# Latent attention with a pair's keys in one tile and each head's score products in half of TensorE's rows

## What is computed

```python
k_eff = (Wdq.T @ Wuq.T @ Wuk).reshape(nh, hs, Lkv)          # nh = 16, hs = 16, Lkv = 64
v_eff = (Wuv.T @ Wo.T).reshape(Lkv, nh, hs).transpose(1, 0, 2)
c_kv = x @ Wdkv.T
q = (x @ Wdq.T @ Wuq.T).reshape(B, T, nh, hs).transpose(0, 2, 1, 3)
q_lat = jnp.einsum('bhtd,hdl->bhtl', q, k_eff)
scores = jnp.einsum('bhtl,bsl->bhts', q_lat, c_kv) / jnp.sqrt(jnp.float32(hs))
scores = jnp.where(causal[None, None, :, :], scores, jnp.finfo(scores.dtype).min)
attn = jax.nn.softmax(scores, axis=-1)
ctx = jnp.einsum('bhts,bsl->bhtl', attn, c_kv)
y = jnp.einsum('bhtl,hld->bhtd', ctx, v_eff)
```

## Time and profile before

| | |
|---|---|
| median of 3 runs | 925.1 us (924.72 to 926.01) |
| profiled execution, first to last instruction (its span) | 923.3 us |
| TensorE busy | 832.7 us, 90% of the span |
| VectorE busy | 766.5 us, 83% |
| ScalarE busy | 605.9 us, 66% |
| GpSimd busy | 430.6 us, 47% |
| latent attention in the span | about 660 to 866 us |

### The profile page before, as it was taken

How to read it: one execution, slowest core, us unless ns; L and a number is a source line. 1 busy time by engine, 2 the same in 40 slices (tenths; PEclk the granted TensorE clock), 3 DMA queues, 4 the chain that set the end, 5 groups by cost and what they waited for, 6 DMA issues and landing times.

```text
span 923.3 us, 13156 instructions
## 1 busy us (share of the span) xinstructions
PE 832.7 (90%) x4330; PEld 534.6 (58%) x4330; DVE 766.5 (83%) x1597; ACT 605.9 (66%) x1042; POOL 430.6 (47%) x455
## 2 busy tenths in 40 slices
PE   3889999999999999989899998679788999998997
PEld 2555665665665565655565565457555555554686
DVE  3788999889989999999899998585598687876637
ACT  5677767777777676766667767374545767657531
POOL 3134354354445277787667771171323434433301
PEclk9999999999999999999999999799989999999999
DMA  3388858966977667857857668130000000000001
GB/s 122 78 184 156 143 117 190 163 126 136 206 134 153 130 131 144 166 110 144 157 103 132 136 130 159 24 106 0 1 1 1 1 0 2 0 2 1 1 1 45
DMA packets 276867, 86.29 MB, mean 93 GB/s; under 512 B 267584, under 2 KB 272448, under 8 KB 276416
## 3 DMA queue, kind: packets, MB, share of 16 engines
q1 hardware_dynamic: 275520, 80.05, 44.8%
q0 software_dynamic: 992, 5.34, 1.9%
q10 hardware_dynamic: 288, 0.07, 0.0%
HBM read 17.29 MB, written 1.05 MB: 20 GB/s over the span
## 4 chain that ended last, share of the span: by engine, by line
PE 40%; DVE 37%; issue 9%; ACT 8%; DMA 3%; POOL 1%; SPq 1%; POOLq 0%; DVEq 0%; ACTq 0%
DVE EP L1762 9%; DVE nmax L1747 8%; PE ps L1097 7%; PE ps L1099 7%; PE ps L1098 7%; PE ps L1120 4%; DVE ptm L1861 3%; PE ps L1358 3%; PE ps L1344 3%; PE ps L1135 3%; PE ps L1323 3%; DVE ps L1947 2%; DMA ET<-EP 2%; DVE OL L1821 2%; DVE st L1661 1%
## 5 line engine op out<-in xcount | busy, mean ns | idle before, releaser
L1523 ACT ACTIVATE EP<-ps,rinv 128x1024 f16<-128x1024 f32 x128 | 142.2, 1112 | 44.5 <-DVE rinv L1757 42.9
L1762 DVE SCALAR_TENSOR_TENSOR EP<-ps,rinv,EP 128x1024 f16<-128x1024 f32 x128 | 163.3, 1276 | 2.4 <-ACT EP L1523 2.0
L1513 ACT ACTIVATE ps<-ps,nmax 128x1024 f32<-128x1024 f32 x128 | 139.2, 1088 | 35.7 <-DVE nmax L1747 35.2
L1747 DVE TENSOR_REDUCE nmax<-ps 128x1 f32<-128x1024 f32 x128 | 155.0, 1211 | 0.7 <-PE ps L1099 0.7
L1097 PE MATMUL ps<-KH,QH 128*128 128x512 f32 x256 | 115.4, 451 | 8.3 <-DVE KL L1729 4.2
L2106 POOL TENSOR_TENSOR wgu<-wgu,ptm 128x688 f32<-128x688 f32 x60 | 99.7, 1661 | 45.8 <-DVE ptm L1861 43.7
L1097 PE MATMUL ps<-ET,VH 128*128 128x512 f16 x256 | 98.7, 385 | 17.8 <-DMA ET<-EP 14.2
L1099 PE MATMUL ps<-KH,QL 128*128 128x512 f32 x256 | 100.8, 394 | 0.0
L2106 POOL TENSOR_TENSOR wdn<-wdn,ptm 128x512 f32<-128x512 f32 x45 | 57.7, 1282 | 92.2 <-DVE ptm L1861 91.0
L1098 PE MATMUL ps<-KL,QH 128*128 128x512 f32 x256 | 100.5, 392 | 0.0
L1098 PE MATMUL ps<-ET,VH 128*128 128x512 f16 x256 | 98.3, 384 | 0.0
(11 more groups left out here) (250 smaller groups left out, 2126.7 us busy)
## 6 DMA issues: line engine op xcount, KB each, us to landing
wqr<-in_wqk SPq DMA_DIRECT2D x16, 256.0 KB, 3.6
wgu<-in_tern POOLq DMA_DIRECT2D x3, 1024.0 KB, 6.1
wvr<-in_wv SPq DMA_DIRECT2D x8, 256.0 KB, 3.9
wor<-in_wo SPq DMA_DIRECT2D x16, 128.0 KB, 3.1
ET<-EP SPq DMA_TRANSPOSE x128, 4.3
X<-in_x SPq DMA_DIRECT2D x2, 512.0 KB, 5.7
prw<-in_down_idx POOLq DMA_DIRECT2D x2, 256.0 KB, 7.0
tern<-in_l_wuq_rep SPq DMA_DIRECT2D x1, 512.0 KB, 4.5
```

The source lines that it names most:

```text
L1513: e.activation(bank, bank, ACT.Exp, bias=nmax[:, c:c + 1], scale=1.0, accum_out=rsum[:, c:c + 1]).then_inc(exped.sem, 1)
L1523: e.mul(EP[:, n % NE_RING, 0, :], SB(u, j), rinv[:, c:c + 1]).then_inc(e_hi.sem, 1)
L1747: e.tensor_reduce(nmax[:, c:c + 1], SB(u, j), AX.X, ALU.max, negate=True).then_inc(maxed.sem, 1)
L1762: e.scalar_tensor_tensor(out=EP[:, n % NE_RING, 1, :], in0=SB(u, j), scalar=rinv[:, c:c + 1], in1=EP[:, n % NE_RING, 0, :], op0=ALU.mult, ...
```

## The change

KT becomes eight tiles of 128 x 1024, one for each pair, from the same four tensors. A pair's keys are one tile, with the even head in rows 0 to 63 and the odd head in rows 64 to 127, like its queries. Each score product reads the 64 rows of its head alone, for weights and stream both, and names the half of the array's rows that it uses (`tile_position`). The fills with zeros and the waits for them go, each key split is one instruction of 128 rows, and the wait for old keys goes, since no pair's tile is used again by another pair. The tiles of `GL` are now those of pairs 0 to 3, and the fill at L2181 waits for their heads.

```diff
@@ order_of_ffn0, order_of_latent
-             ("fold_k", 1), ("keys_zero", 3), ("split",), ("fold_v",), ("turn_in", b1, 1),
+             ("fold_k", 1), ("split",), ("fold_v",), ("turn_in", b1, 1),
...
-    todo += [("hidden", 6, 1), ("turn_in", b2, 0), ("hidden", 7, 1), ("keys_zero", 0), ("keys_zero", 1),
-             ("split",), ("point", "ffn0"), ("reuse", "ffn0")]
+    todo += [("hidden", 6, 1), ("turn_in", b2, 0), ("hidden", 7, 1), ("split",), ("point", "ffn0"), ("reuse", "ffn0")]
...
-    todo += [("point", "latent"), ("keys_zero", 2), ("stats", 2, 0, 6, 2), ("latent", 0, 0), ("stats", 2, 1, 4, 2)]
+    todo += [("point", "latent"), ("stats", 2, 0, 6, 2), ("latent", 0, 0), ("stats", 2, 1, 4, 2)]
@@ build
-        KT = [QH, QL, KH, KL]
+        KT = [t[:, i, :] for t in (KL, QH, QL, KH) for i in range(2)]
...
-        GL = [KT[m // 2][:, m % 2, :] for m in range(4)]
+        GL = KT[0:4]
...
+        def rows_of(h):
+            return slice(64 * (h % 2), 64 * (h % 2) + 64)
@@ TensorE: row_max, weights, weights3
-                    e.matmul(ps[:, i, 0:n], QT(p)[:, i8 * P:i8 * P + P], KT[p % 4][:, hh, c:c + n],
-                             start=True, stop=True).then_inc(max_scored.sem, 1)
+                    e.matmul(ps[:, i, 0:n], QT(p)[rows_of(h), i8 * P:i8 * P + P], KT[p][rows_of(h), c:c + n],
+                             start=True, stop=True, tile_position=(64 * hh, 0)).then_inc(max_scored.sem, 1)
...
-                        e.matmul(ps[:, i, 0:n], KT[p % 4][:, h % 2, k * P:k * P + P], Q2[p % 4][:, q0:q0 + n],
-                                 start=True, stop=True).then_inc(weighed.sem, 1)
+                        e.matmul(ps[:, i, 0:n], KT[p][rows_of(h), k * P:k * P + P], Q2[p % 4][rows_of(h), q0:q0 + n],
+                                 start=True, stop=True, tile_position=(64 * (h % 2), 0)).then_inc(weighed.sem, 1)
...
-                    e.matmul(ps[:, i, 0:n], KT[p % 4][:, h % 2, k * P:k * P + P], Q2[p % 4][:, hi - n:hi],
-                             start=True, stop=True).then_inc(weighed.sem, 1)
+                    e.matmul(ps[:, i, 0:n], KT[p][rows_of(h), k * P:k * P + P], Q2[p % 4][rows_of(h), hi - n:hi],
+                             start=True, stop=True, tile_position=(64 * (h % 2), 0)).then_inc(weighed.sem, 1)
@@ VectorE: key split of pair 0
-                        w.wait_ge(*zeroed["keys", 0, 1])
-                        for hh in range(2):
-                            rows = slice(64 * hh, 64 * hh + 64)
-                            e.tensor_tensor(KT[0][rows, hh, cs], R2[rows, r2, :], f32(R1[rows, r, :]),
-                                            ALU.subtract).then_inc(k_split_v.sem, 1)
+                        e.tensor_tensor(KT[0][:, cs], R2[:, r2, :], f32(R1[:, r, :]),
+                                        ALU.subtract).then_inc(k_split_v.sem, 1)
@@ GpSimd: keys_zero (goes), key split of the other pairs, fill of the last block's weights
-            def keys_zero(step, i):
...
-                    e.memset(f32(KT[i][rows, hh, :]), 0.0).then_inc(zeroed.sem, 1)
...
-                    for hh in range(2):
-                        rows = slice(64 * hh, 64 * hh + 64)
-                        if hh == 1:
-                            w.wait_ge(*k_split_g[2 * p, half])
-                        if p > 3:
-                            w.wait_ge(*weighed[2 * p + hh - 8, 7, "last"])
-                        else:
-                            w.wait_ge(*zeroed["keys", p, 1])
-                        e.tensor_tensor(KT[p % 4][rows, hh, cs], R2[rows, r2, :], f32(R1[rows, r, :]),
-                                        ALU.subtract).then_inc(k_split_g.sem, 1)
+                    e.tensor_tensor(KT[p][:, cs], R2[:, r2, :], f32(R1[:, r, :]),
+                                    ALU.subtract).then_inc(k_split_g.sem, 1)
...
-                    for h in range(8, 12):
+                    for h in range(4 * (m // 2), 4 * (m // 2) + 4):
                         w.wait_ge(*weighed[h, 7, "last"])
```

More of the change, by code:

```diff
@@ L571, in build, with k_split @@
         HEADS, FFN0, LATENT, FFN1 = order_of_heads(), order_of_ffn0(), order_of_latent(), order_of_ffn1()
-        def k_split(h, half):
-            return (k_split_v if h < 2 else k_split_g)[h, half]
+        def k_split(p, half):
+            return (k_split_v if p == 0 else k_split_g)[p, half]
         def added(t):
@@ L868, in build @@
                     zeroed.mark("ones")
[L869 to L872, removed]
             elif what == "point":
@@ L899, in build @@
                 turn_in_banks(take_ring, *at)
[L900 to L903, removed]
             elif what == "point":
@@ L928, in build @@
                     take_ring(step, k_lo_in.mark(p, half))
-                    for hh in range(2):
-                        token = (k_split_v if p == 0 else k_split_g).mark(2 * p + hh, half)
-                    r1_free[r] = r2_free[r2] = token
+                    r1_free[r] = r2_free[r2] = (k_split_v if p == 0 else k_split_g).mark(p, half)
             elif what == "row_max":
@@ L1320, in _ @@
                     w.wait_ge(*q_split[p, i8 // 4])
-                    w.wait_ge(*k_split(h, 0))
-                    w.wait_ge(*k_split(h, (c + n - 1) // 512))
-                    e.matmul(ps[:, i, 0:n], QT(p)[:, i8 * P:i8 * P + P], KT[p % 4][:, hh, c:c + n],
-                             start=True, stop=True).then_inc(max_scored.sem, 1)
+                    w.wait_ge(*k_split(p, 0))
+                    w.wait_ge(*k_split(p, (c + n - 1) // 512))
+                    e.matmul(ps[:, i, 0:n], QT(p)[rows_of(h), i8 * P:i8 * P + P], KT[p][rows_of(h), c:c + n],
+                             start=True, stop=True, tile_position=(64 * hh, 0)).then_inc(max_scored.sem, 1)
                 elif what == "shift":
@@ L2018, in stats @@
                 e.tensor_tensor(nb[:, o, ts], nm[:, o, ts], rs[:, o, ts], ALU.mult).then_inc(ln_shift.sem, 1)
-            def keys_zero(step, i):
[L2021 to L2026, removed]
-                    if hh == 1:
-                        w.wait_ge(*zeroed["keys", i, 0])
-                    e.memset(f32(KT[i][rows, hh, :]), 0.0).then_inc(zeroed.sem, 1)
             e.memset(mhalf[:, :], -0.5).then_inc(half_set.sem, 1)
@@ L2122, in _ @@
                     e.memset(vx4[:, :, :, 0], 1.0).then_inc(zeroed.sem, 1)
-                elif what == "keys_zero":
-                    keys_zero(step, *at)
                 elif what == "split_q":
```

## The result

The changed kernel takes 940.69 us (median of 4 runs, 939.28 to 944.67) against 925.56 (924.72 to 928.47) for the kernel before: a ratio of 1.017, 95% interval 1.0142 to 1.0199. It is slower by 15.1 us. The forecast was 921.9, with a range of 915 to 931: the wrong side, and outside the range.

What follows compares the result with a forecast made beforehand. TensorE was taken to bound the latent attention. GpSimd splits -1.25, dense stretches -1.25, loose +0.2, last group -1.0 and before the first combine +0.1 sum to -3.2: 921.9 us from 925.1, range 915 to 931.

Steps and rivals of the forecast that it cites:

- a rival with a chance of 0.06: Clock rival: half-used rows bring a 1.1 us low-clock visit into each of eight loose stretches, 8.8 us lost, 930.7; chance 0.06.
- loose stretch: One of 8 stretches between combines where TensorE waits for banks that VectorE and ScalarE free; forecast +0.2 us for all.
- The prediction's own sign of being wrong: Latent attention: a granted clock under 1.00 between 717 and 836 would show the forecast wrong.
- Zeroing: Eight GpSimd fills of 0.946 us go, 7.6 us; nothing waited for them, so 0.
- pair 0's split: First pair's key split on VectorE: four half-height subtractions become two full ones; bounds 0 and -1.4 us, taken as 0.
- Key splits on GpSimd: 28 instructions on 64 rows become 14 on 128; two combines waiting behind splits get shorter, -1.25 us.
- Mode switches: TensorE changing between 64-row score products and 128-row work: 0.20 us each, 4.0 us in dense stretches, 8.4 in loose.
- dense stretches: The 13 stretches after combines 0 to 3 of each group and 4 of the last; switches and overlap net -1.25 us.
- Overlap: Neighbouring score products on opposite row halves stream at once; three quarters saved, 6.5 us in dense stretches, 8.0 in loose.
- no overlap: Case in the slower rival: opposite halves save no streaming and switches cost in full, +7.85 us, 932.9; no separate chance.
- the halves load in turn: Slower rival: the second half's weight load is not taken beside the first, +3.1 us, 928.2; chance 0.26.
- The last group: Stretches between combine3 steps: switches 0.6 us against overlap 3.7, a third counted because ScalarE is busy: -1.0 us.

Runs made afterwards that it cites:

- the twins: 64 rows early, plus before each early score product the other head's same-width product on the other half, into an unread bank; against the kernel before: 935.77 us, ratio 1.0117.
- The kernel with 64 rows early: Changed kernel with score products on 128 rows until two banks come free just behind the eighth projection, then on 64; against the kernel before: 940.74 us, ratio 1.017.

## Why the prediction was wrong

**The step that failed** is the granted clock. The forecast's sum has no term for it: it was made at a clock of 1.00 throughout, and the clock stands only in a rival with a chance of 0.06, for which no reason is given (no row of before tied the clock to rows). That rival was too small as well. It sized a visit to the low clock as 1.1 us, by the one between 712 and 716, which had begun before 712 (0.85 from 708 to 712), and put one into each loose stretch, 8.8 us in all. The stage had a longer visit before the change: the clock was 0.62 from 668 to 677, and from 660 to 668, just before it, TensorE was busy 3.66 of 8 us. The longest visit in the changed kernel holds at 0.50 from 704 to 732, 28 us, and lies where I expected nothing: ahead of the first combine. There the sum had +0.1, because VectorE was busy 20.88 of 23.59; measured, the way from the first projection to the first combine is 6.9 us longer. That cover was read at a clock of 0.93; at 0.67 TensorE is marked busy 36.82 of 39.82 us there. The prediction's own sign of being wrong came with it: a clock of 0.82 from 717 to 836 in the changed kernel. What to learn from it: when a cover is named, ask also at which clock it holds.

Of the loss, taken against the kernel with all products on 128 rows (17.3 us by the same stretches), the clock makes the most part: 2.4 ahead of the eighth projection and 5.4 up to the first combine, and the kernel with 128 rows up to the first combine has neither, with the twins giving back 4.9 of the 5.4 at 64 rows; 2.2 from the first combine to the last of the group (31.52 against 29.35 at full clock). In the 5.5 us ahead of the second and third groups' first combines (17.53 and 21.83 against 16.23 and 17.60), about 1 us each would be switches by the 0.96 above. The kernel with 64 rows early points to less: its two stretches at other clocks, carried on in a straight line to 1.00, give 16.6 and 17.9 us, so 0.3 to 0.4 us each. Both are estimates; the rest goes with the clock. These sizes are of one execution each, and the changed kernel's was its slowest: what the medians give back for the early part is 5 us, where the stretches give 10.

**Zeroing** at 0 and **pair 0's split** between 0 and -1.4: nothing speaks against them. From the first to the eighth projection 20.97 us became 20.78 with all products on 128 rows.

**Key splits on GpSimd** at -1.25: right, 1.30 on the two combines with all products on 128 rows.

**Mode switches** at 0.20 us each: right in kind (0.36 by "issue" at 738.80), more than half too dear. On the path a new one costs 0.12 to 0.13 in the dense stretches, and 1.79 us in nine of the thirteen stands against the 4.0 for all. I had said that a loss there arrives whole.

**Overlap** at three quarters: opposite halves do start together, so "no overlap" and "the halves load in turn" fell. What arrives in the same nine stretches is 2.14 us; with the switches it nets -0.35, where the sum had -1.25 for thirteen. The loose stretches, at +0.2 for all eight, were too low by 0.3 to 1 us each at full clock, by the two that were sized. The bound for all of the overlap (916.5) takes the dense stretches' gain whole, where the forecast halves it; halved it would be some 918.9. The last group at -1.0 gained nothing: from its first combine3 to the start of its last 25.52 us became 25.74. ScalarE issues ten exponentials there without a gap in 5.06 us after as in 5.07 before, so I take it to set the pace; no run tests this.

**The rival that came nearest in time**, "no overlap at all" (932.9), is still 8 us short and would have been near for a wrong reason: the overlap is there.

## What to carry to other kernels

A product that uses half of TensorE's rows is not free of consequences because it streams as fast: here it took the engine from 2.4 to 1.2 GHz for 28 us without a break, and zeroed halves, which look like waste, kept it fast. Before products are made smaller, look at the stretches in which little else runs on TensorE, and price them at half clock; a cover by another engine must be checked at that clock too. Where tiles are still wanted, issue both halves together and put products of one mode in a row, since a change of mode costs 0.12 us on the path even where opposite halves win it back.

## What was not expected

Two products on opposite halves of the rows start together to a hundredth of a microsecond, and 66 products added in this way (114 to 180) made a stretch 8.4 us shorter, as its clock went from 0.55 to 1.00. The Trainium skill (TensorEngine Tiling (Array Packing), Theoretical Speedup) gives up to twice the speed for a contraction of 64 rows or fewer; here, at full clock, a group's combines took 29.35 us with it and 29.38 without, and in the nine dense stretches switches took back 1.79 of the 2.14 us that the overlap gave. And TensorE's marked busy time is a poor sign of work done: the stretch at a clock of 0.55 shows 41.24 of 43.32 us busy, the one with more products at 1.00 only 30.97 of 34.88.
